# Context attention: the weighted contexts through value weights and output weights in two steps

## The reference, cut to what matters

```python
q = _split_heads(jnp.einsum('bnd,df->bnf', x, Wq)) * DH ** (-0.5)
kv = jnp.einsum('bmc,cf->bmf', context, Wkv)
k, v = jnp.split(kv, 2, axis=-1)
k, v = (_split_heads(k), _split_heads(v))
k = jnp.concatenate((nk, k), axis=-2)          # one null key and value ahead
v = jnp.concatenate((nv, v), axis=-2)
attn = jax.nn.softmax(jnp.einsum('bhid,bhjd->bhij', q, k), axis=-1)
out = jnp.einsum('bhij,bhjd->bhid', attn, v)
out = out.transpose(0, 2, 1, 3).reshape(b, -1, INNER)
out = jnp.einsum('bnf,fd->bnd', out, Wout)      # 1024 features to 128
...
```

## Time and profile before

| | |
|---|---|
| median of three runs | 4682.25 us (4668.89 to 4694.56) |
| profiled execution | 4693.21 us, first to last instruction 4691.4 us |
| mean granted clock of TensorE | 0.892 |
| TensorE busy in the whole kernel | 3805.9 us, 81% |
| VectorE, ScalarE, GpSimd busy | 2774.1, 2084.6, 875.2 us |
| context attention, first to last matmul | some 88 to 1573 us |
| `c_psO` matmuls (L3758), 1024 records | 482.1 us busy |
| `c_psS` matmuls (L3730), 2048 records | 465.9 us busy |
| `c_psQ` fills (L3715), 1984 records | 261.6 us busy |
| `c_psQ` output (L3770), 2048 records | 233.9 us busy |

### The profile page before, as it was taken

How to read it: one execution, slowest core, us unless ns; L and a number is a source line. 1 busy time by engine, 2 the same in 40 slices (tenths; PEclk the granted TensorE clock), 3 DMA queues, 4 the chain that set the end, 5 groups by cost and what they waited for, 6 DMA issues and landing times. The chain is left out here.

```text
span 4691.4 us, 85272 instructions
## 1 busy us (share of the span) xinstructions
PE 3805.9 (81%) x30810; PEld 2831.4 (60%) x30810; DVE 2774.1 (59%) x5424; ACT 2084.6 (44%) x4510; POOL 875.2 (19%) x840
## 2 busy tenths in 40 slices
PE   7999999999999585279998679899995257869376
PEld 5777878777787354166666356566663135646254
DVE  2555555555555675442223776577777946877783
ACT  2333333333333354544333444378887535654423
POOL 0000000000000131210001036555551022200360
PEclk7999999999999787589998779999997578989667
DMA  3111111111111035220000023222220000000000
GB/s 76 43 55 41 50 46 45 46 45 53 42 50 46 13 113 183 87 100 0 0 0 20 5 114 124 82 72 65 74 65 17 0 5 3 0 13 0 8 2 23
DMA packets 189000, 214.35 MB, mean 46 GB/s; under 512 B 19312, under 2 KB 176976, under 8 KB 181328
## 3 DMA queue, kind: packets, MB, share of 16 engines
q1 hardware_dynamic: 188752, 211.05, 14.4%
HBM read 183.68 MB, written 27.05 MB: 45 GB/s over the span
## 5 line engine op out<-in xcount | busy, mean ns | idle before, releaser
L3758 PE MATMUL c_psO<-c_pt,c_vc 128*128 128x512 f32 x1024 | 482.1, 593 | 2.5 <-ACT c_ot L3845 2.5
L3730 PE MATMUL c_psS<-c_kc,c_qt 128*128 128x257 f32 x2048 | 465.9, 380 | 0.9 <-issue 0.9
L3837 ACT ACTIVATE c_sc<-c_psS,c_mx 128x257 f32<-128x257 f32 x512 | 214.9, 472 | 484.9 <-DVE c_mx L3895 484.9
L3730 PEld LDWEIGHTS c_psS<-c_kc,c_qt 128*128 128x128 f32 x2048 | 381.2, 190 | 66.8 <-issue 17.4
L3884 DVE COPY c_qt<-c_psQ 128x512 f32<-128x512 f32 x248 | 170.5, 687 | 399.9 <-PE c_psQ L3715 399.9
L547 PEld LDWEIGHTS f_psY<-f_w_down,f_hT 128*128 128x128 f32 x2560 | 302.4, 192 | 64.1 <-issue 50.4
L590 ACT ACTIVATE f_hT<-f_psH,f_b_up 128x512 f32<-128x512 f32 x320 | 214.3, 688 | 283.8 <-PE f_psH L537 278.8
L3715 PEld LDWEIGHTS c_psQ<-XT,c_m 128*128 128x128 f32 x1984 | 260.1, 191 | 106.2 <-issue 104.4
L537 PE MATMUL f_psH<-f_xs,f_w_up 128*128 128x512 f32 x640 | 304.6, 612 | 18.3 <-ACT f_hT L590 18.2
L547 PE MATMUL f_psY<-f_w_down,f_hT 128*128 128x128 f32 x2560 | 305.4, 275 | 10.2 <-ACT f_hT L590 7.0
L2223 POOL TENSOR_TENSOR x_sc<-x_sc,x_rec 128x1156 f32<-128x1156 f32 x128 | 270.5, 2113 | 207.4 <-DVE x_rec L2489 207.4
(11 more groups left out here) (794 smaller groups left out, 7675.2 us busy)
## 6 DMA issues: line engine op xcount, KB each, us to landing
c_kc<-in_ctxT SPq DMA_DIRECT2D x128, 257.0 KB, 3.1
c_vc<-in_ctx SPq DMA_DIRECT2D x128, 256.0 KB
g_wide<-g_w_dram SPq DMA_DIRECT2D x32, 1024.0 KB, 8.0
x_kc<-in_ctxT SPq DMA_DIRECT2D x32, 512.0 KB, 4.2
x_vc<-in_ctx SPq DMA_DIRECT2D x64, 256.0 KB
l_k_dram<-l_dist SPq DMA_DIRECT2D x32, 256.0 KB, 3.5
l_q_dram<-l_turn SPq DMA_DIRECT2D x8, 1024.0 KB, 10.0
y_pt<-l_q_dram SPq DMA_DIRECT2D x8, 1024.0 KB, 7.2
```

The source lines that it names most:

```text
L3730: mm = pe.matmul(psS[:, r, 0:KEYS], qt[:, b // BT, half, b % BT, r * G:(r + 1) * G].rearrange("p h i -> p (h i)"), kc[:, b // 2 % 2, b % 2 ...
L3758: mm = pe.matmul(psO[:], vc[:, slot, c % 2, t, half * P:(half + 1) * P], pt[:, c % 2, t], start=(t == 0), stop=(t == 1))
L3837: act.activation(sc[:, b % 2, r, 0:KEYS], psS[:, r, 0:KEYS], ACT.Exp, bias=mx[:, b % 2, r:r + 1]).then_inc(exp_done, 1)
```

## The change

The output is computed in two steps instead of with the folded weights `c_u`. `head_values` multiplies the context of each head with its 256x64 value weights: even heads write partitions 0 to 63 of `c_psQ`, odd heads 64 to 127, four pairs of heads (32 records of each kind) in one turn of the bank, two turns a group. VectorE copies each turn to `c_vo` (`take_values`). `output` then needs eight matmuls, each for two heads at once, with the plain output weights, and the tail matmul as before.

`TURNS_AT` replaces `FILLS_AT`: each batch has three places for a turn of the bank (after the scores, after half 0 of the context, after half 1), and the table names a fill ("q") or a value turn ("v"); the output stands first in batch 3 instead of batch 2. So `c_psQ` has ten turns and an output a group instead of eight and an output. `c_ot` is doubled, one buffer for each group in flight, since the second value turn comes after the new group's first context copy. `c_u` is still built, in `context_weights` alone, for the last context row. Three DMAs on the sync queue load the value and output weights at the start of the stage, and TensorE waits for them before the first batch.

```diff
-    FILLS_AT = ((0, 0, 2), (2, 1, 2), (5, 0, 2), (7, 0, 1))
+    TURNS_AT = ((("q", 0), ("q", 1), ("q", 2)), (("q", 3), ("q", 4), ("q", 5)),
+                (("v", 0), ("v", 1), ("q", 6)), (None, ("q", 7), None))
+    TURNS = FILLS + 2
...
-        ot = sb("c_ot", [P, 2, H16, BT, S])
+        ot = sb("c_ot", [P, 2, 2, H16, BT, S])
+        wv = sb("c_wv", [P, 2, H16, DV])
+        wo = sb("c_wo", [P, H16 // 2, D])
+        vo = sb("c_vo", [P, H16 // 2, P])
...
+        def before(i, b, first):
+
+            if first and b < BT:
+                return FILLS
+            return (i * 2 + b // BT) * TURNS + FILLS - 2
...
                 sp.dma_start(own[:], k.a["own_tail"]).then_inc(fixed, 16)
+                for half in range(2):
+                    sp.dma_start(wv[:, half], k.a["L0_xattn_wv"][half * P:(half + 1) * P]).then_inc(values_loaded, 16)
+                sp.dma_start(wo[:], k.a["L0_xattn_wo_pairs"]).then_inc(values_loaded, 16)
...
-                def output(m, s, fills, fresh):
-                    pe.wait_ge(q_read, fills)
-                    if not fresh:
-                        pe.wait_ge(out_read, m)
-                    pe.wait_ge(ot_ready, (m + 1) * BT * 2)
-                    pe.nop(nofuse=True)
-                    for half in range(2):
-                        for h in range(H16):
-                            pe.matmul(psQ[:, 0:D], ot[:, half, h].rearrange("p b i -> p (b i)"), w["u"][:, half, h],
-                                      start=(half == 0 and h == 0), stop=False)
+                def head_values(s, j):
+
+                    for p in range(4):
+                        for half in range(2):
+                            for e in range(2):
+                                h = (j * 4 + p) * 2 + e
+                                mm = pe.matmul(psQ[e * DV:(e + 1) * DV, p * P:(p + 1) * P], wv[:, half, h],
+                                               ot[:, s, half, h].rearrange("p b i -> p (b i)"),
+                                               start=(half == 0), stop=(half == 1))
+                    mm.then_inc(q_in, 1)
+
+                def output(m, s, read):
+                    pe.wait_ge(q_read, read)
                     pe.wait_ge(lz_ready, m + 1)
                     pe.wait_ge(wn_loaded[s], (m - s) * 32 + 64)
                     pe.nop(nofuse=True)
+                    for p in range(H16 // 2):
+                        pe.matmul(psQ[:, 0:D], vo[:, p], wo[:, p], start=(p == 0), stop=False)
                     pe.matmul(psQ[:, 0:D], lz[:, s].rearrange("p b i -> p (b i)"), wn[:, s], start=False, stop=True)\
                         .then_inc(out_done, 1)
...
+                            pe.wait_ge(q_read, done + turns_done(b % BT, at, opening, filling))
+                            if (kind, j) == ("v", 0):
+                                pe.wait_ge(ot_ready, m * BT * 2)
+                            if (kind, j) == ("q", 7) and not opening:
+                                pe.wait_ge(out_read, m)
+                            pe.nop(nofuse=True)
+                            if kind == "q":
+                                fill(psQ, m + 1, j)
+                            else:
+                                head_values(1 - s, j)
+
+                        turn_of_bank(0)
                         for half in range(2):
                             if not (first and b < 2):
                                 context(i, b, half, first)
-                            if half < late:
-                                queries(j + early + half)
+                            turn_of_bank(half + 1)
                             if half == 0 and not (first and b == 0):
                                 turn(n - 1, (b - 1) % NB)
...
                 pe.wait_ge(fixed, 9 * 16)
+                pe.wait_ge(values_loaded, 48)
...
-                output(NG - 1, 1, NG * FILLS, False)
+                done = before(NI, 0, False) - TURNS + 2
+                pe.wait_ge(ot_ready, NG * BT * 2)
+                for j in range(2):
+                    pe.wait_ge(q_read, done + j)
+                    pe.wait_ge(out_read, NG - 1)
+                    pe.nop(nofuse=True)
+                    head_values(1, j)
+                output(NG - 1, 1, done + 2)
...
-                        if b % BT == 2 and not (first and b == 2):
+                        if b % BT == 3 and not (first and b == 3):
                             output(i * 2 + b // BT - 1)
...
+                def take_values(f, m, j):
+
+                    v.wait_ge(q_in, f + 1)
+                    if j == 0:
+                        v.wait_ge(out_done, m)
+                    v.tensor_copy(vo[:, j * 4:j * 4 + 4].rearrange("p a t -> p (a t)"), psQ[:]).then_inc(q_read, 1)
...
+                        turn_of_bank(0)
+                        turn_of_bank(1)
                         if not (first and b == 0):
                             copy(n - 1, (b - 1) % NB)
                         scale(n, b)
-                        if filling and late == 2:
-                            read(psQ[:], before + j + early + 1, 1 - b // BT, j + early + 1)
+                        turn_of_bank(2)
```

More of the change, by code:

```diff
@@ L3509, in _ @@
                             mm = pe.matmul(bank, last[:, half],
-                                           w["u"][:, half, four * 4:four * 4 + 4].rearrange("p h d -> p (h d)"),
+                                           u[:, half, four * 4:four * 4 + 4].rearrange("p h d -> p (h d)"),
                                            start=(half == 0), stop=(half == 1))
@@ L3523, in _ @@
                         half, four = (j - U_AT) // 4, (j - U_AT) % 4
-                        x = act.activation(w["u"][:, half, four * 4:four * 4 + 4].rearrange("p h d -> p (h d)"),
+                        x = act.activation(u[:, half, four * 4:four * 4 + 4].rearrange("p h d -> p (h d)"),
                                            bank, ACT.Copy)
@@ L3602, in context_attention, with turns_done @@
         out_read = k.sem("c_out_read")
+        def before(i, b, first):
+            if first and b < BT:
+                return FILLS
+            return (i * 2 + b // BT) * TURNS + FILLS - 2
+        def turns_done(b, at, opening, filling):
+            n = 0
+            for bb in range(b + 1):
+                for aa in range(3 if bb < b else at):
+                    use = TURNS_AT[bb][aa]
+                    if use and not (use[0] == "v" and opening) and not (use[0] == "q" and not filling):
+                        n += 1
+            return n
         with nc.Block() as block:
@@ L3721, in scores @@
                     if b % BT == 0:
-                        pe.wait_ge(q_read, (i * 2 + b // BT + 1) * FILLS)
+                        pe.wait_ge(q_read, before(i, b, first))
                     if b % 2 == 0:
@@ L3781, in chunk, with turn_of_bank @@
                         scores(i, b, first)
-                        before = (i * 2 + b // BT + 1) * FILLS
-                        filling = not (last and b >= BT)
-                        j, early, late = FILLS_AT[b % BT]
-                        def queries(j):
-                            if filling:
-                                pe.wait_ge(q_read, before + j)
-                                if j == 5 and not (first and b == 2):
-                                    pe.wait_ge(out_read, i * 2 + b // BT)
-                                pe.nop(nofuse=True)
-                                fill(psQ, i * 2 + b // BT + 1, j)
-                        for e in range(early):
-                            queries(j + e)
-                        if b % BT == 2 and not (first and b == 2):
-                            output(i * 2 + b // BT - 1, 1 - b // BT, before + j if filling else NG * FILLS, first)
+                        m, s = i * 2 + b // BT, b // BT
+                        opening = first and s == 0
+                        filling = not (last and s == 1)
+                        done = before(i, b, first)
+                        def turn_of_bank(at):
+                            use = TURNS_AT[b % BT][at]
+                            if use is None:
+                                if at == 0 and not opening:
+                                    output(m - 1, 1 - s, done + turns_done(b % BT, at, opening, filling))
+                                return
+                            kind, j = use
+                            if kind == "v" and opening or kind == "q" and not filling:
+                                return
+                            pe.wait_ge(q_read, done + turns_done(b % BT, at, opening, filling))
[9 more added lines that the diff above has]
+                        turn_of_bank(0)
                         for half in range(2):
@@ L3844, in context @@
                     act.wait_ge(context_done, n * 2 + half + 1)
[L3845 removed]
+                    act.activation(ot[:, (b - 2) % NB // BT, half, :, (b - 2) % BT], psO[:].rearrange("p (h i) -> p h i", i=S),
```

(26 more changed lines are left out.)

7 lines of the change are left out of this document (5 added, 2 removed).

## The result

The changed kernel takes 4658.17 us (median of 13 runs, 4646.1 to 4673.91) against 4687.89 us for the kernel before (13 runs, among them the three shown ahead). The ratio is 0.9939, interval 0.9927 to 0.995: 28.6 us saved by the ratio, 23 to 34 by the interval (the two medians lie 29.7 apart). The forecast was 42.3 us saved, 4640. The direction was right and the time lies in the stated range of 4618 to 4665, but the gain was a third smaller, and the time lies above the forecast's own range of 4622 to 4656. (The forecast stood on the median of three runs, 4682.25; off the 4687.89 of 13 it would be 4645.6.) The profiled execution of the changed kernel took 4669.11 us.

What follows compares the result with a forecast made beforehand. TensorE bounds the context attention. A group changes by 3.57 + 0.35 + 1.79 − 7.14 = −1.43 us; 31 save 44.3, start and end add 1.2 and 0.8: −42.3 off 4682.25 gives 4640.0, range 4618 to 4665 (own range 4622 to 4656).

Steps and rivals of the forecast that it cites:

- TensorE is the bound and the stage a sum of records: Context attention: TensorE busy 250.00 of 250.00 us; a group sums to 45.7 us of its records, 32 groups make the stage.
- Value turns at half pitch: Head values, 64 records a group: column halves run side by side at 0.0558 us a record, 3.57 us.
- Switches: Into and out of narrow tiles around value turns: four a group cost 0.32 to 0.40 us, taken as 0.35.
- Output, 16 records, 1.79 us: Group's output: eight matmuls, 16 full-width records at 0.1116 us, 1.79 us; the tail matmul stays.
- Start and end: Stage's first group: one more bare gap, +1.2 us; last output alone, 8.0 instead of 7.14 us, +0.8.
- VectorE in time, moves at nothing: Value-turn copies on VectorE (44 us in all) finish before the bank's next use; moved fills, output and copies are covered.
- rival 3: Full drains at the four switches of a group, 0.275 us each: group −0.68 us, kernel 4664; chance 0.05.
- the first: Rival 1, value turns: halves do not overlap, 0.1116 us a record, group +2.14 us, kernel 4754; chance 0.06.
- the second: Rival 2, value turns: half overlap, weight loads set a pitch near 0.08 us, group ±0, 4680 to 4690; chance 0.04.
- the fourth: Rival 4, third turn: VectorE reads too late, TensorE waits 1.15 us a group, group −0.28, kernel 4675; chance 0.05.

## Why the prediction came out as it did

- **TensorE is the bound and the stage a sum of records**: right. No idle time of TensorE from 250 to 1500 us, every group of the same length, and the experiments' groups (47.13, 45.55, 44.14, 45.62) came within 0.9 us of sums made in the same way, three of the four within 0.15.
- **Value turns at half pitch, 3.57 us a group**: right, 2×1.79. I had argued from four narrow tiles in turn against one alone; the run with the halves in blocks shows that both rows were the right ones, each for its order.
- **Switches, 0.35 us a group**: the term of the group that was sized too small. It measured 0.55. I took one way in and one way out from the earlier trace rows, times two. What those rows could not show is that behind a narrow turn the first full-width weight load has no cover either. 0.20×31 = 6 us of the 42 (the group in all fell short by 0.23, 7.1 us).
- **Output, 16 records, 1.79 us**: right, 1.78.
- **Start and end, +1.2 and +0.8**: together 1.2. The group saving of 1.20 times 31 is 37.2, the stage saved 36.0. Counted from the stage's first matmul, the first scores came 0.24 us later, taken as 0; whether that is the wait for the three DMAs was not tried apart.
- **VectorE in time, moves at nothing**: right. Between the turns TensorE waits for no copy; the moves alone changed the group by 0.02 us. (ScalarE's wait for the output was expected to shrink to about 2 us; no idle time is left before it.)
- **The rest of the kernel is untouched**: never written down, and wrong. The sum ended at the stage's last instruction. The stage gave 36.0 us and the kernel 28.6, so 7.4 went elsewhere, 2 to 13 by the interval. The profiles show 4.0 of them, in the m_ stage, behind a barrier at which VectorE's drain came late. The other 3.4 are open: the profiles have some 5 us more behind the m_ stage in the kernels with that drain, but not clear of their scatter, and taking the drain away from the changed kernel lowered its median by only 0.7 us.
- **The range**: met with help. 56 and 28 us saved, taken off 4682.25, give 4626 to 4654, and the prediction said 4622 to 4656; the 4658.17 lies outside both and inside 4618 to 4665 only because that was widened for scatter, up to rival 3. Off the later median of 4687.89 the forecast is 4645.6 and rival 3 some 4670, and the measured time stands about halfway. The time alone does not decide between the two; the rows of the switches do.

Rivals 1 to 4: the first is real for the other order of issue, the second did not occur, the third was nearer than I thought (some 0.3 us for a way in and out, between the 0.175 of the forecast and the 0.55 of the rival), the fourth did not occur.

## What to carry to other kernels

Here narrow matmuls reached half the time only when neighbours in the program used different columns of the array (0.056 against 0.102 us a record), and each visit to the narrow form cost about 0.3 us, so put such work into few long blocks. Where a kernel consists of many stages with barriers, a change of a few instructions moves all later ones, and 0.18 us at one barrier went with 4 us in a stage whose granted clock is not steady. So read the stages behind an edit too, compare the drains at the barriers, and before believing a difference under 0.3% move the streams by some satisfied waits on idle engines.

## What the runs showed of the hardware that I had not expected

- 64-column matmuls in alternation 0.056 us a record, one half at a time 0.102, full width 0.1116.
- Drains of 7 to 19 ns take 123 to 125 (SyncE), 129 to 139 (TensorE) and 136 to 142 ns (VectorE) at single barriers, at places that move with the number of instructions ahead; with the streams 252 to 257 places further on they were gone again. 22 places on VectorE made the one drain slow; 21 did not, in a kernel whose TensorE and SyncE streams were moved too. This fits a stream that is fetched in blocks, which no row shows directly.
- Satisfied waits are not free: 209 on TensorE delayed it by 13.8 us, at least 0.066 each, and 235 on VectorE by 20.6, at least 0.088 each. 30 on VectorE ahead of work that came later anyway cost nothing.
- Identical code from n0y_stats to n1a_psT took 1019.8 to 1034.4 us from run to run. What decides that stays open.
